# Attention product with the early queries' high and low parts packed into one matmul

## The reference

```python
xn = layernorm(x)                                  # x: 4 batches, 256 tokens, 512 wide
q, k, v = xn @ wq, xn @ wk, xn @ wv                # 32 query heads, 8 key/value heads of 128
q, k = rope(q), rope(k)
allowed = (j <= i) & (j > i - 128)                 # causal, sliding window of 128
attn = softmax(where(allowed, q @ k.T * 128 ** -0.5, min))
s = (attn @ v) @ wo
h = silu(xn @ W1.T) * (xn @ W3.T)                  # W1, W2, W3 unpacked from 4-bit values and scales
out = x + s * silu(h @ W2.T)
```

## Time and profile before

| | |
|---|---|
| median of the runs | 801.83 us |
| the profiled execution | 801.65 us, span 799.9 us |
| PE matmul busy | 795.5 us, 99% of the span |
| DVE, POOL, ACT busy | 561.4 us (70%), 475.6 us (59%), 427.0 us (53%) |
| chain that ended last | PE 99% |
| longest wait of PE | 1.0 us, at the start |
| granted clock of TensorE | 1.00 throughout |

### The profile page before, as it was taken

The page is one execution under the profiler, slowest core; times in us unless marked ns, Lnnn a source line. Parts: engine busy times, 40 slices in busy tenths (PEclk is TensorE's granted clock), DMA queues, the critical chain, the costliest instruction groups (busy, mean ns, idle before and its releaser), DMA issues.

```text
span 799.9 us, 13468 instructions
## 1 busy us (share of the span) xinstructions
PE 795.5 (99%) x3966; PEld 672.8 (84%) x3966; DVE 561.4 (70%) x1634; ACT 427.0 (53%) x1104; POOL 475.6 (59%) x357
## 2 busy tenths in 40 slices
PE   9999999999999999999999999999999999999998
PEld 7888888888888888888888888888888888888887
DVE  7715867668448867767686777777677777767785
ACT  5413313223138675666666565666656566665672
POOL 2103314224256774867487486748757674878997
PEclk9999999999999999999999999999999999999999
DMA  9659525201000400400040040004004000420102
GB/s 280 190 179 269 138 66 159 78 28 53 1 27 14 132 14 1 132 2 14 2 131 13 0 131 0 13 0 131 13 0 125 6 13 0 131 66 0 40 0 107
DMA packets 51908, 54.00 MB, mean 68 GB/s; under 512 B 4128, under 2 KB 33184, under 8 KB 51872
## 3 DMA queue, kind: packets, MB, share of 16 engines
q1 hardware_dynamic: 51728, 53.50, 22.3%
q10 hardware_dynamic: 144, 0.07, 0.0%
HBM read 47.25 MB, written 6.29 MB: 67 GB/s over the span
## 4 chain that ended last, share of the span: by engine, by line
PE 99%; DVE 0%; ACT 0%; issue 0%; POOL 0%; POOLq 0%
PE bank L1349 27%; PE bank L1351 27%; PE bank L1350 27%; PE bank L1540 4%; PE bank L1556 3%; PE bank L1573 2%; PE bank L1574 2%; PE bank L1575 2%; PE bank L1582 1%; PE bank L1580 1%; PE bank L1579 1%; PE bank L1478 1%; PE bank L1398 0%; PE bank L1408 0%; PE bank L1377 0%; PE bank L1403 0%
## 5 line engine op out<-in xcount | busy, mean ns | idle before, releaser
L722 ACT ACTIVATE probs<-probs,nmx 128x128 f32<-128x128 f32 x256 | 100.0, 392 | 63.4 <-DVE nmx L1123 63.3
L457 POOL TENSOR_TENSOR swap<-swap,cst 128x512 f32<-128x512 f32 x80 | 107.9, 1349 | 41.8 <-ACT swap L701 41.8
L1349 PE MATMUL bank<-xh,wih 128*128 128x512 f32 x320 | 127.9, 400 | 0.0
L1350 PE MATMUL bank<-xl,wih 128*128 128x512 f32 x320 | 125.1, 391 | 0.0
L1351 PE MATMUL bank<-xh,wil 128*128 128x512 f32 x320 | 125.1, 391 | 0.0
L1349 PE MATMUL bank<-woh,oh 128*128 128x512 f32 (+1 forms) x260 | 101.0, 389 | 0.0
L1350 PE MATMUL bank<-wol,oh 128*128 128x512 f32 (+1 forms) x260 | 100.7, 387 | 0.0
L1351 PE MATMUL bank<-woh,ol 128*128 128x512 f32 (+1 forms) x260 | 100.5, 387 | 0.0
L405 POOL TENSOR_TENSOR hl<-act_h,hh 128x512 fp32r<-128x512 f32 x22 | 31.6, 1435 | 99.6 <-ACT hh L603 99.6
L461 POOL TENSOR_TENSOR q<-q,swap 128x512 f32<-128x512 f32 x64 | 85.9, 1343 | 6.6 <-DVE q L1098 1.6
L480 POOL TENSOR_TENSOR ph<-ph,cst 128x512 fp32r<-128x512 f32 x32 | 42.5, 1327 | 70.5 <-ACT ph L737 70.5
(11 more groups left out here) (140 smaller groups left out, 2018.4 us busy)
## 6 DMA issues: line engine op xcount, KB each, us to landing
raw<-in_wq SPq DMA_DIRECT2D x32, 256.0 KB, 4.8
raw<-in_wo SPq DMA_DIRECT2D x32, 256.0 KB, 4.9
pk<-in_w SPq DMA_DIRECT2D x44, 128.0 KB, 3.7
sc<-in_s SPq DMA_DIRECT2D x44, 128.0 KB, 3.8
vals<-stage SPq DMA_DIRECT2D x16, 256.0 KB, 2.7
vraw<-vals SPq DMA_DIRECT2D x16, 256.0 KB, 2.9
pk<-in_w SPq DMA_DIRECT2D x11, 256.0 KB, 2.7
sc<-in_s SPq DMA_DIRECT2D x11, 256.0 KB, 3.2
```

Of the source, the lines that this page charges most:

```text
L457: nc.gpsimd.tensor_tensor(v, v, spread(sin.unsqueeze(1), P, 2, SEQ), ALU.mult).then_inc(sin_done, 1)
L722: e = nc.scalar.activation(probs[:, s, c0:c1], probs[:, s, c0:c1], ACT.Exp, bias=nmx[:, s, i:i + 1], scale=-1.0, accum_out=rsum[:, s, i:i ...
L1349: nc.tensor.matmul(out_, sh, mh, start=(i == 0), stop=False)
L1350: nc.tensor.matmul(out_, sh, ml, start=False, stop=False)
```

## The change

In tile 0, query 0 to 63 can see keys 0 to 63 only; the same holds for the first 64 queries of tile 1 against key tile 1 (the triangle). So the rows 64 to 127 of the probabilities are zero there. The change writes the low part of the early queries' probabilities into those rows. One matmul of 256 columns (4 heads by 64 early queries) against `vtwice` (the high part of the first 64 values, in both halves of the partitions) then gives high by high plus high by low, and a second one against `vlow` (their low part, over zeros) gives low by high. The late queries keep three matmuls, of 256 columns. The parts are:

- PE: of the four groups of three 512-column matmuls of a batch, two (t = 0, and the triangle) become five matmuls of 256 columns each.
- ACT: `p_hi` of tile 1 copies the early queries of its upper half to the third slot; `v_twice` makes two copies of 64x512 per step, between the second and the third of the step's last four `exps`.
- DVE: `p_lo` is split for tile 0 and gets one more operation for tile 1; `v_low` makes 64x512 low values per step, behind the first of the last two `both`.
- POOL: `near` multiplies three times 256 columns instead of twice 512; one `memset` at the start.
- `p_hi` and `p_lo` of tile 1 stand ahead of `kq_hi` and `kq_lo` of chunk 2 in every step, which they did only in the last group.
- SP: `load_v` waits for `twice_done` and `low_done` beside `vl_done`.

```diff
             def load_v(g, bp):
                 wait(sp, vl_done, cnt(1, g, bp, -1))
+                wait(sp, twice_done, cnt(1, g, bp, -1))
+                wait(sp, low_done, cnt(1, g, bp, -1))
                 sp.dma_start(vraw[:, bp, :, :], ...).then_inc(v_in[bp], 16)
...
             def near(g, bp, b):
+                pool.wait_ge(ph_done, cnt(4, g, bp, 2 * b + 2))
+                nc.gpsimd.tensor_tensor(late_q(ph[:, 2, :]), late_q(ph[:, 1, :]).bitcast(f32), late, ALU.mult)
+                pool.wait_ge(pl_done, cnt(4, g, bp, 2 * b + 2))
+                nc.gpsimd.tensor_tensor(late_q(pl[:, 2, :]), late_q(pl[:, 1, :]).bitcast(f32), late, ALU.mult)
+                pool.wait_ge(early_hi, cnt(2, g, bp, b + 1))
+                pool.wait_ge(early_lo, cnt(2, g, bp, b + 1))
+                nc.gpsimd.tensor_tensor(early_q(ph[:, 2, :]), early_q(ph[:, 2, :]).bitcast(f32), early, ALU.mult)
...
+            def v_twice(g, bp):
+                wait(act, o_ps, cnt(4, g, bp, 0))
+                nc.scalar.activation(vtwice[0:HALF, :, :], vraw[0:HALF, bp, :, :], ACT.Copy)
+                nc.scalar.activation(vtwice[HALF:P, :, :], vraw[0:HALF, bp, :, :], ACT.Copy).then_inc(twice_done, 1)
...
+            def v_low(g, bp):
+                dve.wait_ge(vh_done, cnt(1, g, bp, 1))
+                wait(dve, o_ps, cnt(4, g, bp, 0))
+                nc.vector.tensor_tensor(vlow[0:HALF, :, :], vraw[0:HALF, bp, :, :],
+                                        vh[0:HALF, bp, :, :].bitcast(f32), ALU.subtract).then_inc(low_done, 1)
...
                 masking(ng, nbp, 0, 2)
                 both(ng, nbp, 0, 0)
+                v_low(ng, nbp)
                 accumulate(g, bp, 2)
...
+                    if t == 0:
+                        nc.tensor.matmul(o_early, vtwice[:, 2 * b, :], early_q(both_h), start=True, stop=False)
+                        nc.tensor.matmul(o_early, vlow[:, 2 * b, :], early_q(both_h), start=False, stop=True)
+                        nc.tensor.matmul(o_late, near_h, late_q(both_h), start=True, stop=False)
+                        nc.tensor.matmul(o_late, near_h, late_q(both_l), start=False, stop=False)
+                        nc.tensor.matmul(o_late, near_l, late_q(both_h), start=False, stop=True).then_inc(o_ps, 1)
+                        continue
```

More of the change, by code:

```diff
@@ L70, in build @@
         cos, sin = cst[:, C_COS:C_COS + SEQ], cst[:, C_SIN:C_SIN + SEQ]
-        causal, plain, far, keep = [cst[:, C_MASK + n * P:C_MASK + (n + 1) * P] for n in range(4)]
+        causal, plain, far, keep, keep_twice = [cst[:, C_MASK + n * P:C_MASK + (n + 1) * P] for n in range(5)]
         ident = cst[:, C_ID:C_ID + P]
@@ L763, in _ @@
             kq_hi(0, 0, 2)
+            v_twice(0, 0)
             halves(0, 0, 4)
@@ L797, in first_step @@
                 kq_hi(0, 1, 4)
-                for h in range(1, GH):
-                    exps(0, 1, 0, h)
+                exps(0, 1, 0, 1)
+                v_twice(0, 1)
+                exps(0, 1, 0, 2)
+                exps(0, 1, 0, 3)
                 for c in range(5):
@@ L843, in step @@
                 p_hi(g, bp, 1, 0)
[L844 to L849, removed]
+                p_hi(g, bp, 1, 1)
+                kq_hi(ng, nbp, 2)
                 halves(ng, nbp, 4)
@@ L859, in step @@
                     weigh(ng, nbp, 0, 1)
+                v_twice(ng, nbp)
                 exps(ng, nbp, 0, 2)
@@ L1151, in v_lo @@
                                         ALU.subtract).then_inc(vl_done, 1)
+            def v_low(g, bp):
+                dve.wait_ge(vh_done, cnt(1, g, bp, 1))
+                wait(dve, o_ps, cnt(4, g, bp, 0))
+                nc.vector.tensor_tensor(vlow[0:HALF, :, :], vraw[0:HALF, bp, :, :], vh[0:HALF, bp, :, :].bitcast(f32),
+                                        ALU.subtract).then_inc(low_done, 1)
             def first_wo_lo(g):
@@ L1207, in _ @@
             v_lo(0, 0)
+            v_low(0, 0)
             cos_part(0, 0, 3)
@@ L1251, in first_step @@
                 both(0, 1, 0, 0)
+                v_low(0, 1)
                 accumulate(0, 0, 2)
@@ L1296, in step @@
                 p_lo(g, bp, 1, 0)
[L1297 to L1302, removed]
+                p_lo(g, bp, 1, 1)
+                kq_lo(ng, nbp, 2)
                 masking(ng, nbp, 0, 0, 1)
@@ L1549, in p_turn @@
                 wait(pe, pl_done, cnt(4, g, bp, 2 * b + r - 1))
+                if r == 1:
+                    wait(pe, early_lo, cnt(2, g, bp, b))
                 for h in range(GH):
@@ L1583, in attend @@
-                    m.then_inc(o_ps, 1)
+                    nc.tensor.matmul(O_B[j % 2][:, :], near_l, both_h, start=False, stop=False)
+                    step_h, step_l = [v[:, bp, 2 * b + 1, :] for v in (vh, vl)]
+                    pe.wait_ge(kept, cnt(4, g, bp, 2 * b + 1))
+                    o_early, o_late = early_q(O_B[j % 2][:, :]), late_q(O_B[j % 2][:, :])
+                    nc.tensor.matmul(o_late, step_h, late_q(ph[:, 2, :]), start=False, stop=False)
+                    nc.tensor.matmul(o_late, step_l, late_q(ph[:, 2, :]), start=False, stop=False)
@@ new lines, in attend @@
+                    pe.wait_ge(kept, cnt(4, g, bp, 2 * b + 2))
+                    nc.tensor.matmul(o_late, step_h, late_q(pl[:, 2, :]), start=False, stop=False)
+                    pe.wait_ge(kept_early, cnt(2, g, bp, b + 1))
+                    nc.tensor.matmul(o_early, vtwice[:, 2 * b + 1, :], early_q(ph[:, 2, :]), start=False, stop=False)
+                    nc.tensor.matmul(o_early, vlow[:, 2 * b + 1, :], early_q(ph[:, 2, :]),
+                                     start=False, stop=True).then_inc(o_ps, 1)
```

58 lines of the change are left out of this document (41 added, 17 removed).

## The result

| | before | changed |
|---|---|---|
| median of the runs | 801.82 us (6 runs, 801.66 to 802.67) | 833.56 us (6 runs, 832.96 to 834.19) |
| ratio, 95% interval | | 1.0395 [1.0383, 1.0406] |
| profiled execution | 801.65 us, span 799.9 us | 834.12 us, span 832.3 us |
| mean granted clock | 1.00 | 0.992 |

The change makes the kernel 4% slower. The forecast was 817.9 us, with a range that ended at 826: the sign and the place are right, the size is half of what came.

A forecast was written before the change was run, and what follows sets the result against it. PE, busy 99% of the span, was taken to bound the kernel; 801.65 - 2.6 saved + 18.7 of stalls gave 817.7 us profiled, 817.9 as the median, range 812 to 826.

The forecast's parts named there:

- PE's part: In attend, five 256-column matmuls replace three of 512, saving 0.083 us per group, 5.3 us at most.
- rival 4: Attend's matmuls on 64 of every 128 columns run slower than 0.120 us: 35 us more, 850; chance 0.04.
- Half of it meets `ol_done`: At out_project, attend b = 1's saving is lost to the ol_done wait; b = 0's is kept, 2.6 us taken.
- What the other engines get, costed at nothing: Added copies and operations on ACT and DVE fit into idle time; cost nothing, with 0 to 3 us for the range.
- The stall of 2.67 us, seven times, 18.7: Next group's weights wait on SP behind low_done; PE stands 2.67 us at that projection in seven groups, 18.7 us.
- The later four chunks come in order behind the first [...] so they add nothing on PE.: The next group's other four weight chunks arrive before later projections need them, adding nothing on PE.
- rival 2: Late weights delay p_hi and near, so PE stands still again at attend b = 0: 7 us, 825; chance 0.11.
- The clock stays at 1.00: PE's granted clock does not fall below 1.00 after the stalls, so no clock loss is in the forecast sum.
- Rival 3: PE runs at half speed some 4 us after each stall, costing 2 us each, 14 in all: 832; chance 0.06.

The follow-up runs named there:

- A: Changed kernel with one line moved: SP issues load_v(g + 1, 1) behind the next group's five weight loads; 801.36 us, ratio 0.9994.
- F: A with one more 256-column matmul in each attend: 803.01 us for b = 0, 801.22 us for b = 1 in another kernel.
- G: A with o_hi of tile 2 ahead of a kq_hi on ACT, o_lo of tile 2 ahead of cos_part 4 on DVE; 798.83 us.
- J: The kernel before the change with only G's new order on ACT and DVE; 802.06 us, ratio 1.0001.
- B: The kernel before the change plus one SP wait: load_v(g + 1, 1) waits for the first two both of step (g, 1); 826.46 us.
- D: Changed kernel with the four query chunks' weights loaded ahead of load_v(g + 1, 1), the key chunk's behind it; 828.14 us, ratio 1.0325.
- C: Changed kernel with 12 unread fp32 matmuls on PE ahead of project(ng, 0) in steps bp = 1; 836.03 us.
- E: D plus C's 12 unread matmuls on PE ahead of project(ng, 0) in steps bp = 1; 821.69 us, ratio 1.0246.

## Why the prediction was wrong

By its own steps:

- *PE's part.* Right in kind. The strided 256-column matmuls of `attend` start 0.12 apart, as the contiguous ones of the earlier trace rows do, so rival 4 is out (its sum should have read 852, 817.7 and 34.6, and not 850). The saving was a third too large: 1.9 us came from `attend` b = 0 and not 2.6 (A). The Trainium skill, "Advanced Engine Details and Errata", section "PSUM Cachelines", says that any non-contiguous access significantly slows matmuls down; by these 0.12 this trace does not agree. The sentence behind it there, which wants every two consecutive elements contiguous, fits the trace. Timeline of PE in an `attend` b = 1 (as the earlier trace rows):

```profile
426.10 0.28 PE L1639 MATMUL bank<-ph,vh 128*128 128x256 f32 x1
426.21 0.28 PE L1640 MATMUL bank<-ph,vl 128*128 128x256 f32 x1
426.33 0.28 PE L1642 MATMUL bank<-pl,vh 128*128 128x256 f32 x1
426.45 0.28 PE L1644 MATMUL bank<-ph,vtwice 128*128 128x256 f32 x1
```

- *Half of it meets `ol_done`.* Right, shown from three sides: F (0.120 us more in b = 1 costs nothing), G (take the wait away, 2.5 us come out) and J (the order alone gives nothing).
- *What the other engines get, costed at nothing.* Nearly right: 1.5 us in two single waits, inside the 0 to 3 left for it. I had read `v_low`'s cover in one step only; in the last ones POOL has products on `acc` beside it. I had also read the 0.68 of the earlier trace rows as `v_lo` with POOL idle. POOL's instruction begins 0.06 us behind that one, at 267.81, and is itself the one that takes longer, 1.77 instead of 1.3; the value was right for `v_low`, beside which POOL is idle in every step from 282 us to the last ones.
- *The stall of 2.67 us, seven times, 18.7.* Right: 19.0, each link where it was put, and B shows that SP's order alone makes it.
- *"The later four chunks come in order behind the first [...] so they add nothing on PE."* This step failed, by 7.2 us. The working of rival 2 followed one path only, the weights over POOL's `lo_in` to `near` and `attend` b = 0, and found 0.4 us in hand; that wait did come, at 0.5 us, in the first group (298.06), and in no other. The dear path is ACT's own: behind the fifth `hi_in` stands not only `p_hi` but every `halves`, `exps` and `o_hi` of the step, 3 us further behind PE than before, and PE is 2.7 us late itself. D takes the late chunks away, and the later waits go with them.
- *The clock stays at 1.00.* This failed too, by some 6 us. Rival 3 had it, at 0.06 and 2 us a stall; it is 1.6 us, behind four of seven. C and E show the cause, E the price.

Added to the forecast of 817.9, either failure alone would give 825.1 or 824.1; I gave each a small chance (0.11 and 0.06) and added neither. In the profiled execution, 834.1 against 817.7, the rest is the 1.5 us of single waits, the 0.7 that the packing did not save, and 0.3 each in the stalls and at the start. Both have one root, the stall: they are what comes with PE standing still for 2.7 us seven times, and were wrongly set apart as rivals to it. C shows in addition that they don't just add: in the groups where the clock falls there are no later waits, and when it is kept up they are there.

What is left open: why the clock fell at some stalls and not at others of the same length (four, two and five of seven in the changed kernel, B and D), how much of the later waits hangs on ACT alone, and the 0.71 us at the last group's `scores`.

## What to carry to other kernels

A wait put in front of a transfer holds up everything behind it on the issuing queue, so read that queue's order first, and issue what has the most time in hand last: here moving one line turned 833.6 us into 801.4. Once a stall of the busiest engine is forecast, price its company in the same sum: the engine that handles the late data in order is late with all its other work as well, and the clock may fall. In a sum with both, check that one does not hide the other. And when a saving is swallowed by a wait, look at which instruction stands ahead of the releaser on its own engine: two swaps gave the swallowed half back.

## What the runs showed of the hardware

- The granted clock fell to 0.50 (1.2 GHz) for 3.4 us at 11 of 21 stalls over three profiles (changed kernel, B, D). PE had been idle for 1.7 to 2.8 us in the 21, and for 1.9 to 2.8 in the 11. The fall came from 0.5 us before PE's restart to 1.2 us after it, and cost 1.6 us where eight 512-column matmuls ran in it. With matmuls in the standstill (C, E) the clock fell at none of 14.
- A 64-partition subtraction on DVE (`v_low`) took 0.68 us alone, as long as the 128-partition one of the earlier trace rows, and 1.78 when it began 0.52 us behind a 128x512 instruction of POOL. It then ended 0.55 us behind POOL's, as the 128-partition one of 1.03 did: what counts is how long POOL's instruction still has to run.
- Keeping the clock up was no gain while other engines were late: the kernel with the clock held at 1.00 (C, 836.0) was slower than the one in which it fell (833.6), and with only one chunk late the same filler gained 6.45 us (E against D).
